# Edge scores of a graph attention layer: the order of two node tables, the form of the row gathers, and who adds, multiplies and sums

## What is computed

```python
out = (x @ Wv + bv).reshape(n, H, HD).transpose(1, 0, 2)      # n 384, H 8 heads, HD 64
e = concatenate([x[src], x[dst]], axis=1) @ Ww + bw           # 6144 x 1024
e = leaky_relu(e.reshape(-1, H, 2 * HD).transpose(1, 0, 2), 0.01)
w = (e @ Wa + ba)[..., 0]                                     # one score per edge and head
mat = full((H, n, n), -inf).at[:, src, dst].set(w)
mat = nan_to_num(softmax(mat, axis=-1))
y = elu(matmul(mat, out)) + residual                          # then a layer norm
```

## Time and profile before

| | before |
|---|---|
| median of three executions | 977.73 us (977.2 to 980.36) |
| the profiled execution's own time | 979.79 us |
| its span, first to last instruction | 978.1 us |
| mean granted TensorE clock | 0.817 |
| busy in the span | PE 700.3, VectorE 480.2, ScalarE 150.2, GpSimd 238.0 us |
| stage | table stage to about 57 us, edge stage to 284.9, read-back and softmax after it |

### The profile page before, as it was taken

The page is one execution under the profiler, slowest core; times in us unless marked ns, Lnnn a source line. Parts: engine busy times, 40 slices in busy tenths (PEclk is TensorE's granted clock), DMA queues, the critical chain, the costliest instruction groups (busy, mean ns, idle before and its releaser), DMA issues.

```text
span 978.1 us, 9513 instructions
## 1 busy us (share of the span) xinstructions
PE 700.3 (72%) x2908; PEld 346.4 (35%) x2909; DVE 480.2 (49%) x2034; ACT 150.2 (15%) x349; POOL 238.0 (24%) x221
## 2 busy tenths in 40 slices
PE   6926423332345807982879986489999999999997
PEld 3412101110124703431355542434444444444442
DVE  2547676676678495448462144632255222222211
ACT  1000000000007711431031100111111111111111
POOL 2047877878830430000000000011101101101100
PEclk9967755555555957995879998589999999999999
DMA  8869999999967039103000000539999999999860
GB/s 307 336 198 245 229 239 228 235 237 232 225 179 257 1 121 400 59 1 129 1 0 1 0 1 12 222 112 393 358 379 357 355 379 358 355 373 360 347 252 34
DMA packets 46213, 208.01 MB, mean 213 GB/s; under 512 B 8128, under 2 KB 12224, under 8 KB 36560
## 3 DMA queue, kind: packets, MB, share of 16 engines
q1 hardware_dynamic: 27920, 150.15, 39.9%
q0 software_dynamic: 18240, 57.23, 24.0%
HBM read 200.45 MB, written 10.05 MB: 215 GB/s over the span
## 4 chain that ended last, share of the span: by engine, by line
PE 54%; DVE 6%; ACT 1%; issue 1%; DMA 0%; DVEq 0%; POOLq 0%
PE bank L785 13%; PE bank L812 10%; PE bank L805 7%; PE bank L697 3%; PE bank L712 3%; PE bank L505 2%; PE bank L619 2%; PE bank L625 2%; PE bank L774 2%; PE bank L500 1%; PE bank L766 1%; PE bank L730 1%; PE bank L727 1%; DVE sm L1089 1%; PE bank L794 1%; PE bank L671 1%
## 5 line engine op out<-in xcount | busy, mean ns | idle before, releaser
L546 PE MATMUL bank<-R 128*128 128x384 bf16 x144 | 51.9, 494 | 148.8 <-DVE R L1166 148.8
L785 PE MATMUL bank<-R 128*64 128x512 f32 x576 | 133.3, 605 | 0.0
L1198 DVE SCALAR_TENSOR_TENSOR R<-R,sm 128x128 f32<-128x128 f32 x384 | 86.0, 288 | 68.0 <-DMA R<-tab_dst,e_i 67.5
L458 POOL DMA_INDIRECT R<-tok_tab,slot_tok x36 | 36.5, 1013 | 324.1 <-DVE slot_f L1555 306.2
L812 PE MATMUL bank<-R 128*128 128x512 f32 x216 | 102.0, 609 | 0.0
L505 PE MATMUL bank<-R,xT_s 128*128 128x512 f32 x168 | 80.5, 640 | 0.0
L412 POOL DMA_INDIRECT R<-tab_dst,e_i x48 | 76.4, 1591 | 15.6 <-issue 13.7
L1567 DVE TENSOR_TENSOR R<-R,bank 128x256 f32<-128x256 f32 x36 | 15.2, 421 | 130.7 <-ACT R L989 130.7
L546 PEld LDWEIGHTS bank<-R 128*128 128x128 bf16 x144 | 13.4, 121 | 182.6 <-DVE R L1166 173.4
L805 PE MATMUL bank<-R 128*64 128x512 f32 x288 | 73.3, 599 | 0.5 <-ACT R L983 0.5
L1561 DVE COPY R<-bank 128x512 f32<-128x512 f32 x36 | 24.9, 691 | 89.8 <-PE bank L774 89.8
(11 more groups left out here) (325 smaller groups left out, 1034.9 us busy)
## 6 DMA issues: line engine op xcount, KB each, us to landing
R<-L_w SPq DMA_DIRECT2D x72, 1536.0 KB, 9.6
R<-L_w SPq DMA_DIRECT2D x2, 3072.0 KB, 15.1
score<-R SPq DMA_DIRECT2D x9, 512.0 KB, 5.0
R<-score SPq DMA_DIRECT2D x3, 1536.0 KB, 10.3
R<-L_Ww SPq DMA_DIRECT2D x2, 2048.0 KB, 11.5
R<-L_W SPq DMA_DIRECT2D x4, 1024.0 KB, 8.8
tab_src<-R SPq DMA_DIRECT2D x3, 516.0 KB, 3.6
tab_dst<-R SPq DMA_DIRECT2D x3, 516.0 KB, 3.8
```

Source lines behind the costliest of these rows:

```text
L458: pool.indirect_dma_start(out=xg[j], out_offset=None, in_=tok_tab[:, :], in_offset=bass.IndirectOffsetOnAxis(ap=slot_tok[:, i:i + 1], axis=0),
L546: last = pe.matmul(pb[s][:, 0:N], oh[:, e % 2, 0, P * s:P * s + P], oh[:, e % 2, 1, :], start=(e == 0), stop=(e == ET - 1))
L785: last = pe.matmul(pb[4 + i % 2][halves[h], :], xeT[i % 2][:, k, halves[h]], w13[(2 * i + h) % NWB][:, k, :], start=(k == 0), stop=(k == K ...
L1198: go(stt(lsc[:, P * h:P * h + P], ga[j][:, P * h:P * h + P], 0.0, waR, ALU.max, ALU.mult, accum_out=w_e3[:, t, h:h + 1]))
```

## The change

The source table is made first and entirely, then the destination table, and each has three row buffers, one per tile. GpSimd gathers the source rows of edge tiles 0 to 12 while the destination table is made, into 13 buffers. Destination rows get six buffers of their own and a plain gather; VectorE adds the two rows (1032 floats), multiplies all eight heads in one instruction, ScalarE sums each head in an instruction of its own, and VectorE adds the linear part one tile later. One scatter is under way at a time, and the duplicate test looks at its own tile only. The score fill moves from SyncE's queue, where it stood between table stores, to the front of GpSimd's, right after the constants; the three fills of the other array move behind the last table store.

```diff
-NGA = 6
+NGF = 13
+NGD = 6
...
-        ab = [r1(16320 + ROW * j, ROW) for j in range(2)]
-        ga = [r1(10240 + ROW * j, ROW) for j in range(NGA - 2)] + ab
-        lsc = r1(14400, 1024)
+        dup_s = R2[:, 1024:1536]
+        prod = [R2[:, 1536:2560], r1(ROW * NGD, 1024)]
+        lsc = prod[0]
+        ab = [R2[:, 2560 + ROW * j:2560 + ROW * j + ROW] for j in range(NT)]
+        ga = [r1(10240 + ROW * j, ROW) for j in range(7)] + [R2[:, 12288 + ROW * j:12288 + ROW * j + ROW] for j in range(6)]
+        gd = [r1(ROW * j, ROW) for j in range(NGD)]
...
@@ SyncE @@
-                sp.dma_start(tab_src[P * t:P * t + P, :], ab[0]).then_inc(S("src_rows_stored"), 16)
+                sp.dma_start(tab_src[P * t:P * t + P, :], ab[t]).then_inc(S("src_rows_stored"), 16)
+            for t in range(NT):
                 sp.wait_ge(S("dst_rows_ready"), 2 * t + 2)
-                sp.dma_start(tab_dst[P * t:P * t + P, :], ab[1]).then_inc(S("dst_rows_stored"), 16)
-                if t == 0:
-                    ...
-                    for q in range(9):
-                        sp.dma_start(fill[q], ga[0][:, 0:1024]).then_inc(S("score_filled"), 16)
+                sp.dma_start(tab_dst[P * t:P * t + P, :], ab[t]).then_inc(S("dst_rows_stored"), 16)
+            sp.wait_ge(S("no_token_ready"), 5)
...
@@ GpSimd @@
-            pool.memset(ga[0], NEG).then_inc(S("no_edge_ready"), 1)
...
+            pool.memset(ga[NGF - 1], NEG).then_inc(S("no_token_ready"), 1)
+            pool.wait_ge(S("no_token_ready"), 5)
+            for q in range(9):
+                pool.dma_start(fill[q], ga[NGF - 1][:, 0:1024]).then_inc(S("score_filled"), 16)
...
             def gather_src(t):
-                j = t % NGA
-                if t >= NGA:
-                    pool.wait_ge(S("w_ready"), t - NGA + 1)
+                j = t % NGF
+                if t == NGF - 1:
+                    pool.wait_ge(S("score_filled"), 16 * 9)
+                if t >= NGF:
+                    pool.wait_ge(S("rows_added"), t - NGD + 1)
...
-            def add_dst(t):
-                j = t % NGA
-                pool.wait_ge(S(f"edge_rows{j}"), 32 * (t // NGA) + 16)
-                pool.indirect_dma_start(out=ga[j], out_offset=None, in_=tab_dst[:, :],
-                                        in_offset=bass.IndirectOffsetOnAxis(ap=dst_i[:, t:t + 1], axis=0),
-                                        compute_op=ALU.add).then_inc(S(f"edge_rows{j}"), 16)
+            def gather_dst(t):
+                j = t % NGD
+                if t >= NGD:
+                    pool.wait_ge(S("rows_added"), t - NGD + 1)
+                pool.indirect_dma_start(out=gd[j], out_offset=None, in_=tab_dst[:, :],
+                                        in_offset=bass.IndirectOffsetOnAxis(ap=dst_i[:, t:t + 1], axis=0)).then_inc(S(f"edge_rows{j}"), 16)

             def scatter_score(t):
                 pool.wait_ge(S("w_ready"), t + 1)
-                if t >= 2:
-                    pool.wait_ge(S(f"scores_stored{t % 2}"), 16 * (t // 2))
+                if t:
+                    pool.wait_ge(S("scores_stored"), 16 * t)
...
-            for t in range(4):
+            for t in range(NGF):
                 gather_src(t)
             pool.wait_ge(S("dst_rows_stored"), 16 * NT)
+            for t in range(4):
+                gather_dst(t)
             for t in range(ET):
-                if 4 <= t + 3 < ET:
-                    gather_src(t + 3)
-                add_dst(t)
-                if t >= 3:
-                    scatter_score(t - 3)
...
+                if t >= 1:
+                    scatter_score(t - 1)
+                if t + 4 < ET:
+                    gather_dst(t + 4)
+                if NGF <= t + 4 < ET:
+                    gather_src(t + 4)
+            scatter_score(ET - 1)
...
@@ TensorE @@
+                pe.wait_ge(S("xT_ready"), nth("1", t + 1))
+                for half in range(2):
                     if t:
+                        pe.wait_ge(S("src_half_ready"), 2 * (t - 1) + half + 1)
+                    project(t, 3 + half, xT, Ww[:, 0:4, D * half:D * half + D]).then_inc(S("src_rows_psum"), 1)
+            pe.wait_ge(S("Ww_loaded_dst"), 16)
+            for t in range(NT):
+                for half in range(2):
+                    if t:
+                        pe.wait_ge(S("dst_half_ready"), 2 * (t - 1) + half + 1)
+                    project(t, (5, 0)[half], xT, Ww[:, 4:8, D * half:D * half + D]).then_inc(S("dst_rows_psum"), 1)
...
@@ ScalarE @@
-                    if t and half == 0:
-                        act_.wait_ge(S("src_rows_stored"), 16 * t)
...
+            for t in range(ET):
+                act_.wait_ge(S("prod_ready"), t + 1)
+                for h in range(H):
+                    own = prod[t % 2][:, P * h:P * h + P]
+                    act_.activation(own, own, ACT.Copy, accum_out=w_e3[:, t, h:h + 1]).then_inc(S("heads_summed"), 1)
...
@@ VectorE @@
-                    linear_part(ab[0], half, S("src_rows_ready"))
+                    linear_part(ab[t], half, S("src_rows_ready"))
+            for t in range(NT):
+                dve.wait_ge(S("src_rows_stored"), 16 * NT)
...
+            def add_linear(t):
+                dve.wait_ge(S("heads_summed"), H * (t + 1))
+                tt(w_e3[:, t, :], w_e3[:, t, :], ga[t % NGF][:, 2 * D:ROW], ALU.add).then_inc(S("w_ready"), 1)
...
-                        go(stt(lsc[:, 256 * j:256 * j + P * (j + 1) - lo], keys[:, lo:P * (j + 1)], key_f[:, e:e + 1],
-                               before_s[:, 0:2 * P] if j else tri, ALU.is_equal, ALU.mult, accum_out=dup_f[:, e:e + 1]))
...
+                        go(stt(dup_scr[:, P * j:P * j + P], keys[:, P * j:P * j + P], key_f[:, t + j:t + j + 1],
+                               tri, ALU.is_equal, ALU.mult, accum_out=dup_f[:, t + j:t + j + 1]))
...
-                for h in range(H):
-                    go(stt(lsc[:, P * h:P * h + P], ga[j][:, P * h:P * h + P], 0.0, waR, ALU.max, ALU.mult,
-                           accum_out=w_e3[:, t, h:h + 1]))
-                settle()
-                one(tt(w_e3[:, t, :], w_e3[:, t, :], ga[j][:, 2 * D:ROW], ALU.add))
-                dve.engine_nop().then_inc(S("w_ready"), 1)
+                j = t % NGF
+                if t == 0:
+                    dve.wait_ge(S("first_src_rows"), 16 * NGF)
+                dve.wait_ge(S(f"edge_rows{t % NGD}"), 16 * sum(1 if e < NGF else 2 for e in range(t % NGD, t + 1, NGD)))
+                tt(ga[j], ga[j], gd[t % NGD], ALU.add).then_inc(S("rows_added"), 1)
+                dve.wait_ge(S("rows_added"), t + 1)
+                if t >= 2:
+                    dve.wait_ge(S("heads_summed"), H * (t - 1))
+                stt(prod[t % 2].rearrange(heads, h=H), ga[j][:, 0:2 * D].rearrange(heads, h=H), 0.0, bc(waR[:, None, :], [P, H, P]),
+                    ALU.max, ALU.mult).then_inc(S("prod_ready"), 1)
+                if t:
+                    add_linear(t - 1)
+            add_linear(ET - 1)
```

More of the change, by code:

```diff
@@ L282, in _ @@
                 sp.wait_ge(S("src_rows_ready"), 2 * t + 2)
-                sp.dma_start(tab_src[P * t:P * t + P, :], ab[0]).then_inc(S("src_rows_stored"), 16)
+                sp.dma_start(tab_src[P * t:P * t + P, :], ab[t]).then_inc(S("src_rows_stored"), 16)
+            for t in range(NT):
                 sp.wait_ge(S("dst_rows_ready"), 2 * t + 2)
-                sp.dma_start(tab_dst[P * t:P * t + P, :], ab[1]).then_inc(S("dst_rows_stored"), 16)
-                if t == 0:
-                    sp.wait_ge(S("no_edge_ready"), 1)
-                    fill = score.rearrange("n h -> (n h)").rearrange("(q p c) -> q p c", p=P, c=1024)
-                    for q in range(9):
-                        sp.dma_start(fill[q], ga[0][:, 0:1024]).then_inc(S("score_filled"), 16)
[L292 to L295, removed]
+                sp.dma_start(tab_dst[P * t:P * t + P, :], ab[t]).then_inc(S("dst_rows_stored"), 16)
+            sp.wait_ge(S("no_token_ready"), 5)
+            slots = slot_tab.rearrange("(s p e) c -> s p (e c)", s=NT, p=P)
+            for q in range(NT):
+                sp.dma_start(slots[q], slot0[:, :]).then_inc(S("slots_filled"), 16)
             sp.wait_ge(S("V_ready"), NT)
-            for j in range(2):
-                sp.wait_ge(S(f"scores_stored{j}"), 8 * ET)
+            sp.wait_ge(S("scores_stored"), 16 * ET)
             for i in range(NT):
@@ L395, in _ @@
             pool.iota(rec4[:, :, :, 1], pattern=[[P * K3, NT], [1, K3]], base=0, channel_multiplier=K3).then_inc(S("consts_ready"), 1)
+            pool.memset(ga[NGF - 1], NEG).then_inc(S("no_token_ready"), 1)
+            pool.wait_ge(S("no_token_ready"), 5)
+            fill = score.rearrange("n h -> (n h)").rearrange("(q p c) -> q p c", p=P, c=1024)
+            for q in range(9):
+                pool.dma_start(fill[q], ga[NGF - 1][:, 0:1024]).then_inc(S("score_filled"), 16)
             pool.wait_ge(S("edge_idx_ready"), 1)
-            pool.wait_ge(S("score_filled"), 16 * 9)
```

(15 more changed lines are left out.)

38 lines of the change are left out of this document (8 added, 30 removed).

## The result

The kernel after takes 981.64 us, the median of its runs (979.58 to 985.51), against 977.23 for the kernel before in the same comparison: a ratio of 1.0048, 95% interval 1.0036 to 1.0059. It is slower by 0.48%; the medians are 4.4 us apart. (Two of the 20 executions of the kernel before, 1135.57 and 1906.29 us, lie far off and do not enter the ratio.) The forecast was 950.5, with 940 to 973 as its range.

A forecast was written before the change was run, and what follows sets the result against it. Bound by GpSimd's three DMA instructions (4.52 us a tile) and 99.4% full DMA engines. Start 71.3, ten tiles to 108.7, 35 x 3.91 to 245.6, tail to 257.7 against 284.90: -27.2, so 950.5 us; range 940 to 973.

The forecast's parts named there:

- Start: Table stage: ba at 32.8, source table stored at 44.7, destination gathers from 65.6, first tile at VectorE about 71.3.
- hidden price: Table stage: the nine fills, now ahead of the small loads, delay ba by about 10 us, to 32.8.
- VectorE: Edge stage: addition 1.22 us, multiplication 1.21, in all 3.6 us a tile against 4.52.
- ScalarE: Edge stage: each head's sum takes 0.40 us, 3.2 us a tile.
- rival 4: Edge stage: ScalarE becomes the bound at 0.615 us a sum, 4.96 a tile; time 1007; chance 0.05.
- One scatter: Edge stage: lone scatter's wait behind two gathers allows period P of 3.5 us a tile, hidden by GpSimd's 3.91.
- Rival 2: Edge stage: plain gathers land at 5.8 us all along, period 4.3 a tile; time 972; chance 0.09.
- Rival 3: Edge stage: scatter wait takes over entirely, scatters landing in 6.3 us, 6.4 a tile; time 1077; chance 0.05.
- The prediction's own sign of being wrong: Edge stage: the forecast is wrong if GpSimd's L420 waits for a scatter in most tiles.
- The tail: Edge stage's end: after the last sums one last scatter of 2.2 us, to 257.7; tail 3 us longer than before.
- GpSimd at 3.91: Edge stage: two plain gathers and a scatter, 2 x 1.283 + 1.346 = 3.91 us for each of 35 tiles.
- rival 5: Edge stage: VectorE's instructions lock out GpSimd's DMA instructions, 1.1 us more a tile; time 990; chance 0.05.

The follow-up runs named there:

- runs 4, 5: Kernel after, GpSimd issuing the nine score fills only when ba has landed: 979.69 us with one scatter under way, 961.10 us with two.
- run 6: Kernel after with two scatters under way and only eight source gathers ahead of the destination gathers, fill still on GpSimd: 958.81 us.
- run 1: Kernel after with two scatters under way instead of one, duplicate test over two tiles again: 960.56 us, ratio to before 0.9791 to 0.9877.

## Why the prediction was wrong, by its own steps

In short: with one scatter at a time, GpSimd waits in a loop that the prediction priced at 3.5 us a tile, out of sight behind GpSimd's own 3.91, and that took 4.65. Read-back was forecast at 257.7 and came at 288.04. The 30.3 us lie in three places: 0.7 up to scatter 8 (109.37; the round that it opens was put at 108.7), 25.7 in the 35 three-instruction tiles (162.6 against 136.9), and 3.9 behind them (16.0 against 12.1).

- **Start**: right in the main. ba was put at 32.8 (32.29), the first source gather at 44.7 (44.21). Destination stores landed in 7.1, not the 3.6 taken from the source store: the thirteen gathers run beside them. That put the first destination gather 3.6 and the first addition 2.4 us late. The claim that the fill's collision with ba is a hidden price of its own was not borne out: with thirteen early gathers (runs 4, 5) ba came 8.2 and 9.4 us sooner and the first destination gather within 0.7 us of where it was, so there the transfers set the start. Only with eight did the late ba show (run 6).
- **VectorE**: right. 1.23 and 1.225 (1.22, 1.21), and 3.65 us a tile up to scatter 8 (3.6).
- **ScalarE**: 0.295, and eight sums in about 2.4 us, not 3.2; mis-sized to the safe side, and rival 4 falls.
- **DMA**: q0 at 71.4% of the engines at 110 to 260 us, about the 80% said.
- **The step that failed is "One scatter".** P was put at (2.83 + L) / 2 = 3.5, hidden by GpSimd's 3.91: 2.63 from a scatter to the source gather behind it, L = 4.1 for that gather's landing, 0.2 for the next scatter to land behind it, and nothing for GpSimd to go on. Measured over the 34 rounds up to scatter 43: 2.78 (some instructions are held), 5.4, and 1.1 from that landing to GpSimd's next start: (2.78 + 5.4 + 1.1) / 2 = 4.64, against 4.65. The 1.1 are two parts. In the round above, the gather of 154.14 landed after 5.7, at 159.8; the record that GpSimd's queue leaves when its wait is over stands at 160.1, and the scatter began at 160.84:

```profile
DMA to landing us min/median/max: 5.7/5.7/5.7
L423 POOLq MOVE  x1: 29/29/29, 160.1 to 160.1; - x1
```

  The first part, 0.3, was forecast as 0.2. The second, the hand-over back to GpSimd, 0.7 to 0.8 from the end of the wait to the instruction, stood at nothing; it is there in 29 of the 34 rounds, also where the row says "issue", so the waits are more than the 20.3 us under the scatter's name. In the prediction's own form, the landing alone would give 4.1 and the hand-over alone 3.9; only together do they leave 3.91 clearly behind.
- **Why L was too small.** Rival 2 calls the two gathers of the earlier trace rows "the only plain gathers in the trace". They were not: the source gathers of the edge stage are plain too, and the kernel before has 38 of them at 85 to 260 us. Their landing, on engines 99.4% busy, reads

```profile
DMA to landing us min/median/max: 5.5/6.1/6.9
```

  4.1 is also the lowest value that taking out the store allows (5.7 - 1.6). Rival 2 (L = 5.8, P = 4.3, time 972) had the landing and not the hand-over, and reached two thirds of the way. Rival 3 had the right mechanism, the wait taking over, at a landing of 6.3; by its own price (0.1 more than the landing) it decides from 3.8 and not 4.3, and with two under way scatters landed in 4.4 (run 1, median). What happened lay between the two, and had no chance of its own. The prediction's own sign of being wrong, waits at most scatters, is what came.
- **The tail** was priced for one last scatter. With one under way, the last scatters form a chain, 3.0 to 3.1 from each to the next, and it ends 7.5 us after VectorE.
- **GpSimd at 3.91**: 4.12 even with two scatters, so rival 5's hold exists, at a fifth of the 1.1 us a tile it was priced at. It is not the cause of the slowdown: with two scatters it is there too, and that kernel is 17 us faster than before.

The Trainium skill, "SBUF — State Buffer", section on its two sides, has a VectorE instruction with two SBUF inputs and a GpSimd instruction that reads SBUF exclude each other for whole instructions, and names descriptor writing as a victim of VectorE's two-port modes. The traces agree with the exclusion where an addition is under way (held until about its end) and show next to nothing for whole products and heads, whose second operand is a short repeated row; half products hold by 0.10 on average, and why they do and whole ones don't is open. "DMA: Bandwidth & Descriptors" (anatomy of one DMA on the GpSimd path) puts a transfer's fixed part at about 2 us, most of it the confirmed write; the 2.3 us from the last scatter to SyncE's read-back fit that, the 3.1 between scatters of GpSimd do not without the hand-over.

Of the 4.4 us between the medians, 2.6 are there at the row maxima. The other 1.8 can't be placed with one profile of each kernel, whose clocks differ at 615 us.

## What to carry to other kernels

An engine that waits for its own last transfer pays for everything queued between: the landing of the gather ahead of it, its own landing behind that, and the time to go on after the wait. Before allowing only one in flight, take each of those numbers at its worst row, from all the rows of that kind, and if the room left is smaller than their spread, keep two. Before a stage begins, work out both ends: when the last result is ready, and when the last byte has moved. Moving a transfer helps only the one of the two that is late.

## What the runs showed of the hardware that was not expected

- GpSimd's indirect DMA instruction, usually 0.94 to 1.02 us, took up to 2.05 when it began just behind a VectorE addition of 1.23 us with both inputs in SBUF, and almost nothing more behind a product of the same length. The extra time was what was left of the addition, less about 0.12. With halves of 0.69 us the holds were shorter and more (4.27 us of GpSimd a tile instead of 4.12).
- A scatter of eight floats a row lets SyncE go on 2.3 us after its start, but GpSimd itself only after 3.0 to 3.1: its queue's record shows the wait over 0.7 to 0.8 before its instruction begins.
- A plain gather landed in 5.4 us with its queue at 71% of the engines, slower than the 4.1 estimated from two gathers beside a store by taking the store out.
- In one program, with an array and nine fills more, ScalarE's sums came late with nothing shown to wait for (31.5 us in 160, 53 times); the cause is open.
